# Order of the first node loads, statistics and edge chunks in a graph-network kernel

## What is computed

```python
xn = layernorm(x)                                   # mean and variance of each node's 256 features
out1 = segment_sum(edge_attr, dst); out2 = segment_max(edge_attr, dst); out3 = out1 / count
h = relu(concat([xn, out1, out2, out3, u]) @ W1 + b1) @ W2 + b2          # graph network
q, k, v = split(xn @ W_qkv + b_qkv)                                      # normalised linear attention
kv = einsum('bnc,bnd->bcd', norm(k*k), v);  attn = (v + norm(q*q) @ kv / sqrt(N)) @ W_out + b_out
x = x + (h + xn) + attn
x = x + processed(layernorm(x))       # two-layer network on the half of the nodes of largest weight
```

## Time and profile before

| | us |
|---|---|
| median of three runs | 1195.56 (1194.41 to 1196.45) |
| the profiled execution's own time | 1192.08 |
| its span, first to last instruction | 1190.3 |
| TensorE busy in the span | 1013.1 (85%) |
| VectorE busy | 1015.5 (85%) |
| ScalarE busy | 485.9 (41%) |
| GpSimd busy | 464.7 (39%) |
| first statistics to last statistics | 14.24 to 45.2 |
| chunk 0, chunk 1, chunk 2 begin | 22.15, 50.76, 60.53 |

### The profile page before, as it was taken

The page is one execution under the profiler, slowest core; times in us unless marked ns, Lnnn a source line. Parts: engine busy times, 40 slices in busy tenths (PEclk is TensorE's granted clock), DMA queues, the critical chain, the costliest instruction groups (busy, mean ns, idle before and its releaser), DMA issues.

```text
span 1190.3 us, 15796 instructions
## 1 busy us (share of the span) xinstructions
PE 1013.1 (85%) x4561; PEld 759.5 (64%) x4561; DVE 1015.5 (85%) x2405; ACT 485.9 (41%) x1439; POOL 464.7 (39%) x344
## 2 busy tenths in 40 slices
PE   3288889999987578059999999999999995899996
PEld 1155555656645455047888888888888982488885
DVE  6899999999999999969888889888897858576574
ACT  3557766777842244002322333223332333243341
POOL 0088840888400000476654446644443000223331
PEclk9598989999995879569999999999999996599998
DMA  9899999999988999632433334433243130111110
GB/s 320 311 317 373 347 356 356 358 363 364 346 312 319 401 415 377 243 86 67 156 121 126 120 99 155 132 123 129 81 138 111 54 116 18 37 36 41 46 43 20
DMA packets 95984, 236.02 MB, mean 198 GB/s; under 512 B 13122, under 2 KB 68711, under 8 KB 89651
## 3 DMA queue, kind: packets, MB, share of 16 engines
q1 hardware_dynamic: 50450, 157.00, 35.7%
q10 hardware_dynamic: 31248, 44.71, 10.5%
q0 software_dynamic: 14224, 33.61, 10.0%
HBM read 154.72 MB, written 80.55 MB: 198 GB/s over the span
## 4 chain that ended last, share of the span: by engine, by line
PE 51%; DVE 4%; issue 1%; POOL 1%; DMA 1%; ACT 0%; DVEq 0%; POOLq 0%
PE psR L67 5%; PE psQ L56 5%; PE psQ L57 5%; PE psQ L58 5%; PE psC L67 5%; PE psKx L56 5%; PE psKx L57 5%; PE psKx L58 5%; PE psR L68 3%; PE psC L68 2%; PE psT L2046 1%; PE psQ L2067 1%; PE psKx L2067 1%; PE psR L66 1%; PE psC L66 1%
## 5 line engine op out<-in xcount | busy, mean ns | idle before, releaser
L459 POOL DMA_INDIRECT graw<-in_edge_attr,ic x98 | 143.1, 1461 | 74.7 <-DVE ob L981 39.4
L978 DVE SCALAR_TENSOR_TENSOR ob<-ob,mQ,mx 128x96 f32<-128x96 f32 x392 | 123.0, 314 | 4.4
L981 DVE SCALAR_TENSOR_TENSOR ob<-ob,kQ,xb 128x96 f32<-128x96 f32 x392 | 122.7, 313 | 0.1
L661 POOL DMA_INDIRECT near<-ends_d,blki x49 | 87.7, 1790 | 71.9 <-DVEq L886 57.3
L661 POOL DMA_INDIRECT near<-in_dst,rowi x49 | 87.8, 1793 | 59.7 <-DVEq L895 45.1
L1721 ACT ACTIVATE hT_hi<-psQ 128x512 fp32r<-128x512 f32 (+2 forms) x52 | 29.9, 575 | 182.9 <-PE psQ L2067 182.9
L1863 PE MATMUL psQ<-Wqk,xT 128*128 128x512 f32 (+1 forms) x196 | 96.8, 618 | 0.0
L966 DVE TENSOR_TENSOR xb<-xb 128x1536 f32<-128x1536 f32 x49 | 86.1, 1758 | 1.7
L964 DVE TENSOR_TENSOR mx<-xb 128x1536 f32<-128x1536 f32 x49 | 85.7, 1748 | 1.1
L1721 ACT ACTIVATE hT_hi<-psKx 128x512 fp32r<-128x512 f32 (+2 forms) x52 | 29.9, 575 | 90.9 <-PE psKx L2067 90.7
L67 PE MATMUL psR<-W2w,hT_hi 128*128 128x512 f32 x175 | 64.2, 404 | 2.8 <-DVE x L1133 2.8
(11 more groups left out here) (499 smaller groups left out, 3230.6 us busy)
## 6 DMA issues: line engine op xcount, KB each, us to landing
xb<-in_edge_attr SPq DMA_DIRECT2D x49, 1536.0 KB, 11.1
scan_d<-ob SPq DMA_DIRECT2D x49, 768.0 KB, 6.3
yrow_d<-yr SPq DMA_DIRECT2D x48, 132.0 KB
xg<-in_x ACTq DMA_DIRECT2D x12, 512.0 KB, 11.8
xT_d<-xT ACTq DMA_DIRECT2D x12, 512.0 KB, 8.8
base_d<-dcur ACTq DMA_DIRECT2D x12, 512.0 KB
qT_d<-qT ACTq DMA_DIRECT2D x12, 512.0 KB, 9.7
out_x<-xres SPq DMA_DIRECT2D x48, 128.0 KB
```

Of the source, the lines that this page charges most:

```text
L459: nc.gpsimd.indirect_dma_start(out=to.rearrange("p i f -> p (i f)"), out_offset=None, in_=raw_v, in_offset=bass.IndirectOffsetOnAxis(ap=ic ...
L661: nc.gpsimd.indirect_dma_start(out=near[:, t, :], out_offset=None, in_=table, in_offset=bass.IndirectOffsetOnAxis(ap=rows[:, t:t + 1], axi ...
L978: nc.vector.scalar_tensor_tensor(o[:, q, 0:EF], prev[:, 0:EF], mQ[:, bass.ds(c * TQ + q, 1)], mx[:, q, 0, :], ALU.min, ALU.max).then_inc(s ...
L981: nc.vector.scalar_tensor_tensor(o[:, q, EF:AGG], prev[:, EF:AGG], kQ[:, bass.ds(c * TQ + q, 1)], X[:, q, 0, :], ALU.mult, ALU.add).then_i ...
```

## The change

Three lists are changed; no instruction is added or taken away but one wait. SyncE issues node groups 0 and 1 in front of `dcur` and `dprv`; then chunk 0, groups 4 to 7, chunk 1, the end table, groups 8 to 11, chunks 2 and 3 and the last group. VectorE clears its tiles first, takes the statistics of groups 0 to 3 before it waits for the target nodes, and runs chunk 1 and `blocks_of_last_edges` between the second and the third quarter of the statistics. ScalarE's queue issues groups 2 and 3 only, and its weight loads stand behind a new wait for the first 16 tiles' statistics.

```diff
             @block.sync
-                sp.dma_start(dcur[:, :], dcur_v).then_inc(s_dst, 16)
-                sp.dma_start(dprv[:, :], dprv_v).then_inc(s_dst, 16)
...
+                def nodes_in(h):
+                    for e in range(4):
+                        sp.wait_ge(s_stat, (h * 4 + e - 3) * GT)
+                        sp.dma_start(xs[e][:, :, :], x_group(h * 4 + e, GT, P)).then_inc(s_xs[e], 16)
+                for e in range(2):
+                    sp.dma_start(xs[e][:, :, :], x_group(e, GT, P)).then_inc(s_xs[e], 16)
+                sp.dma_start(dcur[:, :], dcur_v).then_inc(s_dst, 16)
+                sp.dma_start(dprv[:, :], dprv_v).then_inc(s_dst, 16)
                 edges_in(0)
+                nodes_in(1)
+                edges_in(1)
                 sp.wait_ge(s_tbl, 1)
                 sp.dma_start(ends_d..., part_ends[:, :]).then_inc(s_tbo, 16)
-                for h in range(1, 3):
-                    for e in range(4):
-                        sp.wait_ge(s_stat, (h * 4 + e - 3) * GT)
-                        sp.dma_start(xs[e][:, :, :], x_group(h * 4 + e, GT, P)).then_inc(s_xs[e], 16)
+                nodes_in(2)
+                for b in range(2, XB):
+                    edges_in(b)
                 sp.wait_ge(s_stat, (GROUPS - 3) * GT)
                 sp.dma_start(xs[0][0:LAST, 0:1, :], x_group(GROUPS, 1, LAST)).then_inc(s_xs[0], 16)
-                for b in range(1, XB):
-                    edges_in(b)

             @block.vector        (L787 to L815, unchanged, become the function edge_flags)
-                dve.wait_ge(s_dst, 32)
...
+                def edge_flags():
+                    dve.wait_ge(s_dst, 32)
...
                 stats_quarter(0)
+                edge_flags()
                 row_ends()
                 keep_flags()
                 edge_chunk(0, 0, 0)
                 bias_row()
                 stats_quarter(1)
+                edge_chunk(1, 1, 0)
+                blocks_of_last_edges()
                 stats_quarter(2)
                 stats(GROUPS, 1, LAST, xs[0], s_xs[0], 64)
                 query_bias()
                 variances()
                 deviations()
-                for c in range(1, CHUNKS):
+                for c in range(2, CHUNKS):
                     edge_chunk(c, c % XB, c // XB)
-                    if c == 1:
-                        blocks_of_last_edges()

             @block.scalar
-                for e in range(4):
+                for e in range(2, 4):
                     act.dma_start(xs[e][:, :, :], x_group(e, GT, P)).then_inc(s_xs[e], 16)
+                act.wait_ge(s_stat, 4 * GT)
                 act.dma_start(Wqk[:, :, :], ...).then_inc(s_wload, 16)
```

More of the change, by code:

```diff
@@ L533, in edges_in @@
                                  ev[:, b * T:(b + 1) * T, :]).then_inc(s_load[b], 16)
-                edges_in(0)
-                sp.wait_ge(s_tbl, 1)
-                sp.dma_start(ends_d.rearrange("a b -> (a b)").rearrange("(p j) -> p j", p=P), part_ends[:, :]).then_inc(s_tbo, 16)
-                for h in range(1, 3):
+                def nodes_in(h):
                     for e in range(4):
@@ L542, in _ @@
                         sp.dma_start(xs[e][:, :, :], x_group(h * 4 + e, GT, P)).then_inc(s_xs[e], 16)
+                for e in range(2):
+                    sp.dma_start(xs[e][:, :, :], x_group(e, GT, P)).then_inc(s_xs[e], 16)
+                sp.dma_start(dcur[:, :], dcur_v).then_inc(s_dst, 16)
+                sp.dma_start(dprv[:, :], dprv_v).then_inc(s_dst, 16)
+                edges_in(0)
+                nodes_in(1)
+                edges_in(1)
+                sp.wait_ge(s_tbl, 1)
+                sp.dma_start(ends_d.rearrange("a b -> (a b)").rearrange("(p j) -> p j", p=P), part_ends[:, :]).then_inc(s_tbo, 16)
+                nodes_in(2)
+                for b in range(2, XB):
+                    edges_in(b)
                 sp.wait_ge(s_stat, (GROUPS - 3) * GT)
                 sp.dma_start(xs[0][0:LAST, 0:1, :], x_group(GROUPS, 1, LAST)).then_inc(s_xs[0], 16)
-                for b in range(1, XB):
-                    edges_in(b)
                 def dump_and_load(c, b, load):
@@ L782, in step @@
                         dve.wait_ge(s_v, nv[0])
-                dve.wait_ge(s_dst, 32)
[L786 to L815, removed]
                 for i in range(4):
                     step(nc.vector.memset(xn[i][:, :, NF:NF + 1], 1.0), False)
+                def edge_flags():
+                    dve.wait_ge(s_dst, 32)
+                    cq = dcur[:, :].rearrange("p (q i) -> p q i", i=4)
+                    pq = dprv[:, :].rearrange("p (q i) -> p q i", i=4)
+                    step(nc.vector.tensor_tensor(kQ[:, :], pq[:, :, 0], cq[:, :, 3], ALU.is_equal), False)
+                    step(nc.vector.tensor_tensor(keepc[:, :], dprv[:, 0:1], dcur[:, R - 1:R], ALU.is_equal))
+                    step(nc.vector.tensor_scalar(mQ[:, :], kQ[:, :], 0.5, 2.0, ALU.subtract, ALU.mult))
+                    step(nc.vector.tensor_scalar(mQ[:, :], mQ[:, :], FMAX, None, ALU.mult))
+                    nc.vector.memset(neutral[0:1, 0:EF], -FMAX).then_inc(s_neutral, 1)
+                    nc.vector.memset(neutral[0:1, EF:AGG], 0.0).then_inc(s_neutral, 1)
+                    nc.vector.memset(ob[1][:, TQ - 1, 0:EF], -FMAX).then_inc(s_max, 1)
+                    nc.vector.memset(ob[1][:, TQ - 1, EF:AGG], 0.0).then_inc(s_sum, 1)
+                    dve.wait_ge(s_const, 3)
+                    step(nc.vector.tensor_copy(node[:, :], nodei[:, :]))
+                    step(nc.vector.tensor_scalar(nhalf[:, :], node[:, :], 0.5, None, ALU.add))
+                    nc.vector.tensor_scalar(diag[:, :], ident[:, :], keepc[:, 0:1], None, ALU.mult).then_inc(s_cbc, 1)
+                    run = mxs[1][:, :, :, :].rearrange("p q h f -> p (q h f)")[:, 0:Q]
+                    step(nc.vector.memset(run, 1.0))
+                    step(nc.vector.tensor_tensor_scan(run, kQ[:, :], run, 1.0, ALU.mult, ALU.mult))
+                    step(nc.vector.tensor_reduce(lead[:, :], run, mybir.AxisListType.X, ALU.add))
+                    step(nc.vector.scalar_tensor_tensor(fixf[:, :], node[:, 0:1], float(Q - 1), lead[:, :], ALU.mult, ALU.add), False)
+                    step(nc.vector.tensor_scalar(fixs[:, :], lead[:, :], 0.0, None, ALU.is_gt))
+                    step(nc.vector.tensor_scalar(fixf[:, :], fixf[:, :], -float(P * Q + 2), None, ALU.add))
+                    step(nc.vector.tensor_tensor(fixf[:, :], fixf[:, :], fixs[:, :], ALU.mult))
+                    step(nc.vector.scalar_tensor_tensor(fixf[:, :], fixf[:, :], float(P * Q + 1), node[:, 0:1], ALU.add, ALU.add))
+                    step(nc.vector.tensor_copy(fixi[:, :], fixf[:, :]))
+                    step(nc.vector.memset(cs[:, 0, 0:1], -FMAX), False)
+                    step(nc.vector.memset(cs[:, 1, 0:1], 0.0), False)
+                    nc.vector.tensor_copy(part_ends[:, :], dcur[:, :].rearrange("p (j b) -> p j b", b=BLK)[:, :, BLK - 1]).then_inc(s_tbl, 1)
```

## The result

The changed kernel takes 1205.62 us (median of 5 runs, 1203.88 to 1210.18); the kernel before, beside it, 1195.56 (5 runs, 1190.72 to 1196.45). The ratio is 1.0103 [1.0082, 1.0125]: slower by about 1%, outside the predicted range. The profiled execution of after took 1205.14 us with a span of 1203.4; before had 1192.08 and 1190.3. So the two traces stand 13.1 us apart, and it is these 13.1 us that are to be found.

The account below looks back on a forecast made before the run. VectorE was taken to bound the kernel up to about 500 us; -0.8 at chunk 2 and +1.3 at `key_norm` gave +0.5 us, moving the median from 1195.56 to 1196.1, range 1192.6 to 1200.4.

Parts of the forecast that it names:

- What bounds the kernel: VectorE bounds up to about 500 us, so whatever moves chunk 2's start moves the end one for one.
- VectorE's start: Before chunk 0: statistics end at 11.7 us, target nodes land at 12.5, chunk 0 starts at 21.3, 0.85 us earlier.
- rival (c): At the start, node rows only exchange one wait for another: chunk 2 at 61.5, +1.0 us, 1196.5; chance 0.57 shared with the forecast.
- `bias_row`: Behind chunk 0: the new wait delays `Wqk` and `uT`, so it runs at 32.1 us, turning 0.85 gain into 0.9 loss.
- the upper bound of 33.9: Latest `bias_row` start, in us, if the weights share with groups 4 to 7 and chunk 1: 2.7 us more.
- To chunk 2: From `bias_row` on: 1.7 us of node waits go, remaining work 27.6 us, chunk 2 at 59.7, 0.8 us earlier.
- the slip: Attention groups come 9.8 us later against VectorE's chunks; group 5's slack of 3.5 leaves a 6.3 us `key_norm` wait.
- The 5 us "regained": On ScalarE, earlier gathers win back a third of the 14.5 us base-row waits, leaving a 1.3 us `key_norm` wait.
- rival (a): The slip is paid in full: `key_norm(5)` waits 4 to 6.3 us, total +4.4, 1200.0 us; chance 0.25.
- -0.8 and +1.3: The forecast's two summed terms in us: chunk 2 starting earlier, and the wait left at `key_norm`; together +0.5.

Follow-up runs that it names:

- the start that the prediction described: Changed kernel with node groups 2 and 3 also on SyncE's queue, in front of the target nodes; ratio 1.0073 [1.0052, 1.0093] against the kernel before.
- the two small moves: Kernel before with `row_ends` and the `crow` copy right behind `diag`, `bias_row` behind the second statistics quarter; ratio 0.995, run again 0.9987 [0.997, 1.0004].

## Why the prediction was wrong

**What bounds the kernel: right.** The last scan step moved by exactly chunk 2's delay plus VectorE's waits behind it (8.9 + 5.4 = 14.3).

**VectorE's start: wrong, and the first error.** The step that failed is the landing of the first loads: all 3.7 MB were sized by bytes, as one stream ("nearer to the first because two queues feed here"), so that "the statistics then end at about 11.7 and are hidden in full". For the target nodes the 12.5 us were good (11.7). But the two groups on ScalarE's queue share with rows 6 and 12 times as wide and land at 13.9 and 18.0; the flags start at 19.34, chunk 0 at 28.05 instead of 21.3. It stood in the trace of before, where group 3, issued at 3.82 us, landed 13.2 later, at 17.0 (issue and landing, KB and us):

```profile
3.82 0.56 ACTq L1412 DMA_DIRECT2D k<-in_x  x1
...
k<-in_x ACTq DMA_DIRECT2D x1, 512.0 KB, 13.2
```

There VectorE came to it at 18.17 and did not wait. The first two groups took 11.9 us against 4.4 for the larger target table. The prediction cites these two numbers in rival (c) and does not use them in the sum; with 12 us for a group issued at 2 the statistics could not have ended at 11.7. "DMA: Bandwidth & Descriptors" in the Trainium skill, section "Queues, rings and completion order", has a rule that fits: each DMA engine takes turns between the queues that have work and changes over only at the end of a packet of several descriptors. The runs agree in so far as the same 512 KB landed 5 to 6 us sooner in wider rows; the size of a packet no run shows. The 358 GB/s that the prediction takes from the section "Bandwidth" of this page of the Trainium skill are the share of a core whose neighbour at the memory is busy too. Only one core works here, and the sum did not use the figure.

**`bias_row`: mechanism right, size wrong.** It does wait for TensorE, and the new wait does hold the weights. But the wait ends with the same late statistics, at 19.4 instead of 11.7, and `uT` takes 8.1 us from its issue to TensorE's start (23.33 to 31.42) instead of 6.1. Together 41.13 instead of 32.1; the upper bound of 33.9 left the first out, since it took the landing of the groups for safe. TensorE's products last 9.7 us, 9.9 before, so nothing else is in it. One reading of the earlier trace rows was too quick: TensorE's start at 21.28 was called the landing of `uT`, but it stands right behind the `keep_flags` products, so 6.1 us was only an upper bound there. It held: with the early copy of `crow` TensorE does wait for `uT`, and starts 6.1 us after its issue. With the changed start it took 8.0 to 10.8, from issue to TensorE's start in after:

```profile
23.33 1.18 ACTq L1435 DMA_DIRECT2D uT<-in_L_gnn_u  x2
...
31.42 1.22 PE L1830 MATMUL psKx<-wrow,ones 1*128 1x257 f32 x2 [4.36 <-DMA uT<-in_L_gnn_u]
```

So this term was too small by itself: with the start that the prediction described, and `uT` issued 1.2 us sooner than it says, `bias_row` still ran at 34.18, behind the bound of 33.9. Why `uT` is slow there is open. Chunk 1's 12 KB rows may be the reason, or the node groups 4 to 7 that SyncE also issues earlier; with only the chunk moved, where its load leaves 4.6 us behind `uT`, it took 6.2.

**To chunk 2: right, but for one term.** The 1.7 us of waits for groups 4 to 11 are gone. The last group, taken as none out of 0 to 0.5 us, waits 1.0 (0.5 to 2.2 in the other kernels with chunk 1 in front of it, 7.0 in the one without). 69.44 - 41.13 = 28.3 us instead of 27.6.

**The attention stage: the slip right, the credit wrong.** The row of `key_norm(3)` in before, behind the last sum it needs:

```profile
140.43 0.19 ACT L1539 ACTIVATION_READ_ACCUMULATOR junk<-q 128x1 f32 x1
...
151.82 0.17 DVE L988 TENSOR_SCALAR rk<-k2s 128x4 f32<-128x4 f32 x1
```

The slack of `key_norm` at groups 0 and 1 fell by 10.6 and 10.4 us (9.8 predicted). The 5 us "regained" are the second step that failed. The gathers did end as early as predicted, the last one issued at 149.1 us (159.8 in before). But ScalarE's waits for the base rows fell from 14.5 (13.5 of it up to group 5) to 10.7 only, and they moved forward: up to the sums of group 3 they were 0.8 + 1.3 + 2.7 = 4.8 us and are now 7.4 + 3.4 = 10.7. Group 3 had 11.2 us of slack before; less 10.5, less the 5.9 more of waits, leaves -5.2, and the wait is 5.4. For group 5 the prediction's 3.5 - 10.5 + 2.8 regained + 5.4 that VectorE had then lost itself gives 1.2, as measured. So the prediction looked at the smallest slack, and not at the one with the waits in front of it: after the slip, group 3's 0.7 was the smaller. That is rival (a)'s size, 4 to 6.3 us, but not its path: the slip was paid at group 3 and not at group 5. In the kernel with only the chunk moved it came to 9.8, 4.4 more than in after. ScalarE waited 2.7 us more there up to those sums (3.6 for another write of its queue, `qT_d`, and 0.9 less for base rows); the other 1.7 us are not accounted for.

**What stays open.** What makes ScalarE wait for the base rows' write. Gathers run beside the attention groups in all kernels. In the one with chunk 1 moved back they start at 81.3 us and hold 13.4 and 14.9% of the DMA engines (100 to 140 and 140 to 180 us), the sums of group 0 end at 86.8, and ScalarE waited for it 0.2 us in all; in before, with nearly the same picture some 17 us earlier (63.6, 12.9 and 12.2%, 70.1), it waited 14.5. Spread rows took the wait away in one execution, so where the gathers read may be a part of it, but it is not the whole. Both its size and the group on which it falls differ between two traces of the same kernel: the one with the two small moves showed 3.6 and 10.8 us, and, run again, 1.6, 2.7 and 7.9. And of the 0.4% between the ratios of after and of the kernel without the new wait, the traces account for 0.1%.

The rest is in the sum: -0.8 and +1.3 were forecast, +8.9 and +5.4 came, less the 1.2 us behind the last scan step that no term explains. With the start as sized, the change would still have been slower: the kernel with the forecast start shows 1.0073 [1.0052, 1.0093].

## What to carry to other kernels

Size a load on a second queue by its rows against the rows beside it, and use its measured landing if the trace has one; here bytes over bandwidth gave the landing of the wide rows, and missed that of the narrow rows on the other queue by more than 5 us. A wait put in front of a queue of loads inherits every lateness of what it waits for, so price it with the upper end of that, not with its forecast. When work of the bounding engine is moved in front of what releases another stage, subtract the slip from the slack of every fixed meeting point, and then the waits in front of each of them; move the meeting points along with it. That is cheap here: in the kernel with the two small moves, two norms set one chunk later moved the last scan step by 0.1 us.

## What the runs showed of the hardware

- A DMA of 512 rows of 1 KB on ScalarE's queue took 11.8 to 16.1 us beside rows of 6 and 12 KB on SyncE's (12.4 and 15.8 in after), 6.1 and 6.9 us with only 1 KB rows beside it, and as 128 rows of 4 KB 7.3 and 9.8 us in the same company.
- `uT`, 0.2 KB and queued behind 1 MB of weights, let TensorE start 6.1 us after its issue in before's order (measured with the early copy of `crow`, where it does wait for `uT`), and 8.0 to 10.8 us after it in the kernels with the changed start in which it waits for `uT`.
- Gathers that read few rows again and again held 15.3% of the DMA engines for 0.62 MB (60 to 100 us) and 11.9% for 0.52 MB (100 to 140 us) in after, and up to 17.7% in other kernels; as many gathers of spread rows held 10.8 and 9.9%. Beside them ScalarE waited 10.7 and 1.5 us for its base rows up to group 3, but 0.2 us in another kernel with the few rows.
